# adaLN attention and FFN block on one core: prologue, epilogue and the place of the q and k projections re-ordered

## What is computed

```python
mod = (_silu(L0_c) @ L0_wmod).reshape(8, 6, 1, -1)
ga = (2 * (ga >= 0) - 1) * maximum(abs(ga), 0.25)  # gb likewise
h = _layernorm(x) * (1 + ca) + sa
q, k, v = (split_heads(lora_linear(h, ...)) for each)
scores = where(causal, q @ k.T / sqrt(16), -inf)
x = x + ga * lora_linear(softmax(scores) @ v, wo, ao, bo)
h = _layernorm(x) * (1 + cb) + sb
w = softmax of h @ Wg.T + bg, the two highest of 4 experts kept
expert_out[e] = relu(h @ Wi.T + h @ A[e].T @ B[e].T) @ Wo.T
x = x + gb * sum over e of w[e] * expert_out[e]
```

## Time and profile before

| | us |
|---|---|
| median of 3 runs | 1964.28 |
| lowest, highest | 1963.49, 1966.62 |
| the profiled execution | 1965.01 |
| its span, first to last instruction | 1963.3 |
| TensorE busy in it | 1801.6 (92%) |
| VectorE, ScalarE, GpSimd busy | 1239.0, 939.6, 530.5 |
| granted TensorE clock, mean | 0.967 |

### The profile page before, as it was taken

The page is one execution under the profiler, slowest core; times in us unless marked ns, Lnnn a source line. Parts: engine busy times, 40 slices in busy tenths (PEclk is TensorE's granted clock), DMA queues, the critical chain, the costliest instruction groups (busy, mean ns, idle before and its releaser), DMA issues. The chain is left out here.

```text
span 1963.3 us, 31621 instructions
## 1 busy us (share of the span) xinstructions
PE 1801.6 (92%) x10868; PEld 943.5 (48%) x10868; DVE 1239.0 (63%) x2681; ACT 939.6 (48%) x1701; POOL 530.5 (27%) x833
## 2 busy tenths in 40 slices
PE   7689879999989999899999999899999999799868
PEld 5334335454544555444554545445554545344535
DVE  3666677757686577666676576765777565863131
ACT  2145555544455445545455445554455454554320
POOL 2012112233223222233222232232222332133313
PEclk9579899999999999999999999999999999899979
DMA  7523243213322223223222233223222132120000
GB/s 177 145 50 87 51 87 83 70 40 78 85 60 71 56 64 87 70 38 92 63 71 70 40 85 70 72 58 82 47 60 79 31 88 63 39 39 25 25 1 22
DMA packets 249862, 128.69 MB, mean 66 GB/s; under 512 B 158214, under 2 KB 244834, under 8 KB 249708
## 3 DMA queue, kind: packets, MB, share of 16 engines
q1 hardware_dynamic: 245564, 125.61, 26.6%
q10 hardware_dynamic: 4144, 1.07, 0.4%
HBM read 83.06 MB, written 41.97 MB: 64 GB/s over the span
## 5 line engine op out<-in xcount | busy, mean ns | idle before, releaser
L1049 ACT ACTIVATE probs<-st 128x512 f32<-128x512 f32 (+1 forms) x1216 | 674.8, 576 | 705.2 <-PE st L896 703.1
L1314 DVE TENSOR_REDUCE negm<-mxs 128x1 f32<-128x384 f32 (+4 forms) x736 | 446.6, 617 | 243.3 <-PE mxs L884 239.1
L896 PE MATMUL st<-q_st,k_st 98*128 98x512 bf16 (+3 forms) x1536 | 452.3, 333 | 25.5 <-ACT probs L1049 18.3
L880 PE MATMUL mxs<-k_st,q_st 96*128 96x512 bf16 (+3 forms) x1280 | 408.1, 329 | 47.0 <-DVE negm_left L1314 26.7
L1314 DVE TENSOR_REDUCE negm_left<-mxs 128x1 f32<-128x512 f32 x512 | 345.2, 687 | 144.6 <-PE mxs L880 142.2
L911 PE MATMUL ov<-probs,v_g 128*32 128x512 f32 (+3 forms) x3072 | 333.2, 506 | 1.2 <-POOL probs L743 1.1
L880 PEld LDWEIGHTS mxs<-k_st,q_st 96*128 96x128 bf16 x1280 | 124.0, 98 | 300.8 <-DVE negm_left L1314 98.6
L855 PE MATMUL dense<-c_t,wi_t 128*128 128x512 f32 x512 | 263.9, 601 | 3.3 <-ACT ratio_b L1107 2.4
L756 POOL TENSOR_TENSOR hid<-hid,second 128x512 f32<-128x512 f32 x128 | 161.7, 1266 | 305.6 <-DVE second L1368 305.6
L896 PEld LDWEIGHTS st<-q_st,k_st 98*128 98x128 bf16 x1536 | 142.3, 99 | 169.1 <-ACT probs L1049 66.1
L740 POOL TENSOR_TENSOR fence<-fence 128x1 f32<-128x1 f32 x256 | 50.2, 196 | 613.8 <-ACT probs L1049 613.7
(11 more groups left out here) (165 smaller groups left out, 1696.4 us busy)
## 6 DMA issues: line engine op xcount, KB each, us to landing
q_st<-q_parts_scratch SPq DMA_DIRECT2D x384, 64.0 KB
k_st<-k_parts_scratch SPq DMA_DIRECT2D x384, 64.0 KB
q_parts_scratch<-q_part SPq DMA_DIRECT2D x16, 768.0 KB, 3.3
k_parts_scratch<-k_part SPq DMA_DIRECT2D x16, 768.0 KB, 5.2
xin<-in_L_attn_x SPq DMA_DIRECT2D x8, 1024.0 KB, 5.9
values_scratch<-v_rows SPq DMA_DIRECT2D x32, 256.0 KB, 2.1
v_g<-values_scratch SPq DMA_DIRECT2D x128, 64.0 KB, 3.9
x<-in_L_attn_x SPq DMA_DIRECT2D x16, 512.0 KB, 4.3
```

Of the source, the lines that this page charges most:

```text
L880: last = nc.tensor.matmul(mxs[:, bank_m, j * n:j * n + left], q_st[0:KS, slot, h0 + j, qt * P:(qt + 1) * P], k_st[0:KS, slot, h0 + j, k0:k ...
L896: last = nc.tensor.matmul(st[:, score_bank(ch, kt, h0), j * n:(j + 1) * n], k_st[0:KS + 2, slot, h0 + j, kt * P:(kt + 1) * P], q_st[0:KS + ...
L1049: nc.scalar.activation(probs[:, par, h0:h0 + heads, 0:n], st[:, score_bank(ch, kt, h0), 0:heads * n].rearrange("p (j q) -> p j q", q=n), A ...
L1314: nc.vector.tensor_reduce(dst[:, h0:h0 + heads], src, axis=AX.X, op=ALU.max, negate=True).then_inc(max_free, 1)
```

## The change

Three things are changed. **Prologue:** the norm of batch 0 (`ls1`, `ln1`) stands ahead of the gates' setup on VectorE; `ps` copies the parts of one half at a time (`ps00`, `ps01`), the first after two projections, and the first group's reads come ahead of the v rows 4 to 7; the maxima use the two score banks beside their own two (`max_room`). **Bodies:** all eight projection tiles stand among the FFN's tiles, four ahead of the first and four after the fifth (`PJ_UNITS` is empty); the copy of `ot` 0 is in unit 26, the load of `x1` in unit 37. **Epilogue:** the dense steps use all eight banks; the statistics of each quarter stand right behind its output projection; five FFN tiles' matmuls with the weights (`fa`, now both halves of the contraction) stand between the routing and the steps that need it, and from there five are kept ahead.

```diff
@@ body_plan @@
-        extra[PS_UNITS[0]] = ("ps", 0, 0)
-        extra[PS_UNITS[1]] = ("ps", 1, 0)
+        for ot in range(2):
+            begins[PS_UNITS[ot]] += [("ps", ot, 0, half) for half in range(2)]
...
-    extra[34] = ("xl", 0)
+    extra[37] = ("xl", 0)
...
-PJ_UNITS = (0, 6, 10, 11, 15)
-PJ_SLOTS = (5, 9, 13)
+PJ_UNITS = ()
+PJ_SLOTS = (0, 1, 2, 3, 9, 10, 11, 12)
-PS_UNITS = (17, 36)
+PS_UNITS = (26, 36)
@@ prologue_plan @@
-    plan = [("su", i) for i in range(N_PROJECTION_SETUP)]
-    plan += chain_steps(("ls1", "ln1")) + [("t1", i) for i in range(4)] + [("xin",)]
+    plan = [("su", 0)] + chain_steps(("ls1", "ln1")) + [("su", i) for i in range(1, N_PROJECTION_SETUP)]
+    plan += [("t1", i) for i in range(4)] + [("xin",)]
     values = [opened("va", i) for i in range(4)]
-    plan += values[0] + values[1] + pj[0] + [("ps", 0, 0)]
-    plan += values[2] + values[3] + [("rs", g, half, g) for g in range(2) for half in range(2)] + [("vg", 0)]
+    plan += values[0] + values[1]
+    for half in range(2):
+        plan += pj[0][4 * half:4 * half + 4] + [("ps", 0, 0, half)]
+    plan += [("rs", 0, half, 0) for half in range(2)] + values[2] + values[3]
+    plan += [("rs", 1, half, 1) for half in range(2)] + [("vg", 0)]
...
-    plan += [("ms",), ("ps", 1, 0), ("nm", 0)] + score_steps(0, *UNITS[0])
+    plan += [("ms",), ("nm", 0), ("ps", 1, 0, 0), ("ps", 1, 0, 1)] + score_steps(0, *UNITS[0])
@@ epilogue_plan @@
-    plan += [s for i in range(4) for s in opened("oa", i)]
-    plan += chain_steps(("ls2", "ln2")) + [("t2", i) for i in range(4)] + [("rt",), ("rx",)] + chain_steps(("ro",))
+    for i in range(4):
+        plan += opened("oa", i) + [("ls2", i)]
+    plan += chain_steps(("ln2",)) + [("t2", i) for i in range(4)] + [("rt",), ("rx",)] + chain_steps(("ro",))
+    tiles = [(half, ft) for half in range(2) for ft in range(8)]
+    plan += [("fa", *t) for t in tiles[:EARLY_TILES]]
     plan += [("mt", v) for v in range(2)] + [("rb", half) for half in range(2)]
     for half in range(2):
-        for ft in range(0, 8, 2):
-            plan += [(name, half, ft + i) for i in range(2) for name in ("fa", "fx")]
-            plan += [("fb", half, ft + i) for i in range(2)]
+        of_half = tiles[8 * half:8 * half + 8]
+        for i, t in enumerate(of_half):
+            plan.append(("fx", *t))
+            n = 8 * half + i - 2
+            if i >= 2:
+                plan.append(("fb", *tiles[n]))
+            if i >= 2 and n + EARLY_TILES < 16:
+                plan.append(("fa", *tiles[n + EARLY_TILES]))
+        for n in (8 * half + 6, 8 * half + 7):
+            plan.append(("fb", *tiles[n]))
+            if n + EARLY_TILES < 16:
+                plan.append(("fa", *tiles[n + EARLY_TILES]))
         plan += [s for t in range(4) for s in opened("wa", half, t)]
+EARLY_TILES = 5
+EPILOGUE_BANKS = 8
@@ adaln_block @@
+        banks = [dense[:, i, :] for i in range(DENSE_BANKS)] + [mxs[:, i, :] for i in range(MAX_BANKS)]
+        banks += [st[:, i, :] for i in range(SCORE_BANKS)] + [ov[:, :]]
+        def max_room(it):
+            spare = [st[:, i, :] for i in range(SCORE_BANKS)] if it < 0 else []
+            return [mxs[:, i, :] for i in range(MAX_BANKS)] + spare
...
-                    bank_m = done("mx") % MAX_BANKS
-                    after(pe, max_free, done("mx") - MAX_BANKS + 1)
+                    room = max_room(it)
+                    out = room[done("mx") % len(room)]
+                    after(pe, max_free, done("mx") - len(room) + 1)
...
                 elif kind == "fx":
                     half, ft = a
-                    hidden(db, 1, half, ft)
+                    if it < NB:
+                        hidden(db, 1, half, ft)
+                    elif (half, ft) == (0, 0):
+                        for i in range(EPILOGUE_BANKS):
+                            after(pe, dense_free[i], done(f"low bank{i}"))
```

More of the change, by code:

```diff
@@ L137, in body_plan @@
     extra = {}
+    begins = {u: [] for u in range(GROUPS * NU)}
     if post:
@@ L325, in tallied, with with_banks @@
     return names
-def with_banks(plan, first):
+def with_banks(plan, first, banks):
     n, steps, open_at = first, [], {}
@@ L333, in with_banks @@
         if s[0] in DENSE:
-            bank = next(i % DENSE_BANKS for i in range(n, n + DENSE_BANKS) if i % DENSE_BANKS not in open_at.values())
+            bank = next(i % banks for i in range(n, n + banks) if i % banks not in open_at.values())
             assert not (open_at and needs_all(s)), (s, open_at)
@@ L342, in with_banks @@
     assert not open_at
-    return steps, n % DENSE_BANKS
+    return steps, n % banks
 def needs_all(step):
@@ L378, in phase @@
                 counts["turned"] = counts["full"]
+            if s[0] in ("mt", "rb"):
+                counts[f"low bank{bank}"] = counts[f"bank{bank}"]
             if s[0] in ("vp", "rx", "t1"):
@@ L866, in run @@
                 db, db_b = dense_bank(bank)
+                if it == NB and kind == "ce":
+                    pe.wait_ge(exp_done, done("qk"))
+                    pe.wait_ge(max_free, done("mx"))
                 if kind == "mx":
@@ L1092, in run @@
                         act.wait_ge(blank_out, 16)
-                    after(act, parts_out[ot], done(f"ps{ot}") * (2 * 16))
+                    after(act, parts_out[ot][half], done(f"ps{ot}{half}") * (2 * 16))
                     nc.scalar.copy(dst[:, 0, :], db[:, :]).then_inc(part1_ready, 1)
```

56 lines of the change are left out of this document (33 added, 23 removed).

## The result

The changed kernel takes 1954.39 us (median of four runs, 1952.20 to 1954.59), against 1965.45 for the kernel before on the same chip (four runs, 1963.49 to 1967.87). By the medians it is 11.1 us faster (a quotient of 0.9944), where 12.2 were forecast, and inside the range of 1941 to 1962. The ratio that compares all runs of both kernels is 0.9927, with a 95% interval of 0.9902 to 0.9953; the quotient of the two medians lies inside it. It was profiled twice. The first profiled execution has a span of 1952.6.

The account below looks back on a forecast made before the run. TensorE was taken to bound attention beside the FFN, chains of single steps the epilogue's end. Terms -4.5, -5.1, +2.8 and -5.4 sum to -12.2, taking the median from 1964.3 to 1952.1 us; range 1941 to 1962.

Parts of the forecast that it names:

- Start of the maxima: Prologue: copying parts to DRAM by halves and the early norm let the reads and first maxima start earlier, -4.5 us.
- Four banks: Prologue maxima: with four banks VectorE runs through without bank waits, 26.6 us in place of 31.7, -5.1 us.
- 24.9 us of work, 0.7 until its first reduction, and about 1 us of seams: Prologue maxima: VectorE's busy time plus start and seams, giving a stretch of 26.6 us in place of 31.7.
- the rival that TensorE is the limit (3): Prologue maxima: TensorE at half clock is the limit, so four banks bring nothing; 1957 us in all, chance 0.06.
- Batches 1 to 6: Bodies: moving five projection tiles later costs +0.3 us per batch, with 1.0 for the clock +2.8 in all (-9 to +12).
- rival (2): Bodies: the clock falls in every batch around unit 14, costing 10 us in all; 1962 us, chance 0.12.
- rival (1): Units 10 to 14: v tiles don't fit under VectorE's chain, 3.0 us more per batch; 1970 us, slower, chance 0.07.
- if the clock row shows half speed in each batch: Bodies: a sign, named beforehand, that the prediction is wrong; no size of its own.
- keep their order: Batches 0 and 7: their order stays as before, so no gain or loss was counted for them.
- Epilogue: Epilogue: -5.4 us in all, from five FFN tiles done early, less +1.4 for later statistics and +3.8 of late waits.
- rival (4): Epilogue and bodies: GpSimd's backlog (3.4 us) and the bodies' losses (0.8 per batch) don't show; 1944 us, chance 0.15.

Follow-up runs that it names:

- the balanced run: Changed kernel with the epilogue's statistics behind all output projections again and later weight tiles split five and six over its halves: median 1950.18 us, ratio 0.9897.

## Why the prediction came out right, point by point

The stages of both kernels, from both pairs of profiles (first boundaries as in the text; us):

| | forecast | first pair | second pair |
|---|---|---|---|
| start of the maxima | -4.5 | 62.66 to 57.93: -4.7 | 62.47 to 58.53: -3.9 |
| maxima | -5.1 | 31.7 to 23.7: -8.0 | 31.7 to 24.6: -7.1 |
| from there to the end of batch 0 | 0 | -3.4 | -4.5 |
| batches 1 to 6 | +2.8 | +4.5 | +7.5 |
| batch 7 | 0 | +4.2 | +0.9 |
| epilogue | -5.4 | -3.2 | -7.2 |
| sum | -12.2 | -10.6 | -14.2 |

The total was right, and in part for reasons that it did not give.

**Start of the maxima: right.** Reads at 48.47 where the bounds were 48.5 and 49.9, first maxima at 57.93 where 58.1 stood. SP's own time was the bound, as the lower end had it: the reads start 0.74 us behind the last copy's issue. The half copies landed in 3.2 and 3.6 us (medians in that stretch), the whole k copy in 4.9. The page DMA: Bandwidth & Descriptors of the Trainium skill (the formula for one DMA) makes 2.9 of a half copy, by a fit to DMAs that GpSimd issues; these are SP's, two under way at a time, and the trace is 0.3 to 0.7 above it. The estimate by it, reads at 48.5 to 49, came true, but the landing did not decide it here; it did with the copies together, where the reads start 0.02 us behind the landing of the first half's k parts.

**Four banks: right mechanism, term too small by 2 to 3 us.** The step that failed is "24.9 us of work, 0.7 until its first reduction, and about 1 us of seams". It takes busy time for a floor. VectorE's reductions overlap in the records, which its timeline shows (two of 0.69 booked as 1.28, the next pair 1.20 later):

```profile
68.74 1.28 DVE L1360 TENSOR_REDUCE negm_left<-mxs 128x1 f32<-128x512 f32 x2
69.94 1.28 DVE L1360 TENSOR_REDUCE negm_left<-st 128x1 f32<-128x512 f32 x2
71.14 1.02 DVE L1360 TENSOR_REDUCE negm<-mxs 128x2 f32<-128x512 f32 x2
```

One reduction of 0.69 comes every 0.60, so the work is less than its busy sum, and the stretch ended 1 us below the 24.9 that stood as its least. The same 41 VectorE records that were busy for 24.89 us with waits between them are busy for 22.92 when they stand close. That the two banks were the cause the run with two banks shows, and the rival that TensorE is the limit (3), so that four banks bring nothing, is out: its 26.2 busy us were its half clock, 18.1 in the changed kernel at 0.86. That the clock would rise with the banks the prediction did not say.

**Batches 1 to 6: three ranges right, one wrong, and rival (2) came true.** Means over batches 1 to 6, per batch: units 0 and 1 -0.40 (forecast -0.4), 6 to 9 -1.09 (-1.0), 10 to 14 -6.20 (-5.5), 17 to 47 +7.70 (+8.1). Batch 7's units were a good model, with the v tiles wholly hidden in units 10 to 14: rival (1) is out. But units 15 and 16 were to be 0.85 shorter and are 0.73 longer. That is rival (2), "The clock falls in every batch around unit 14", which had 0.12 and 10 us in all; 1.6 per batch is 9.5. Half clock stood there for 6.8 to 10.2 us in all six batches, against 3.4 to 6.8 in four of them before (3.4 in four in its second profile). The prediction had named "if the clock row shows half speed in each batch" as a sign that it is wrong, and by that sign it was. That the total still came near is luck: units 10 to 14 and 17 to 47 gave 6 us more than forecast. The runs that put work into unit 15 (half clock mostly 3.4 us per batch, units 15 and 16 3.4 us shorter in all) and into 14 and 15 (no half clock at all) tie it to TensorE's idle time there. What exactly brings it is open: with the same wait of 1.68 us in unit 14 two of the six batches of the kernel before stayed at 1.00.

**Batches 0 and 7: "keep their order" failed as an argument.** Their plans are nearly unchanged, their time isn't. In batch 0 the load of x1, moved by three units, no longer stands ahead of the key reads on SP; putting it back brought 3.7 us in the units behind it. In batch 7 the reads for its first units came 2.1 us later, behind a store that the batch before issues later; that is 0.5 to 1.6 of its 4.2 us, and most of the rest is half clock that the first profile of before did not have and the second did. In neither case had I listed what stands behind the moved step on SP. What the Trainium skill says in DMA: Bandwidth & Descriptors (issuing engines are not separate DMA queues), that another issuing engine saves only issue time, was not tried here; what the reads lost on SP was the store's wait for its data (4.7 us for GpSimd's `ob` ahead of 1634.75), in which SP issues nothing.

**Epilogue: terms right, the base was not typical.** The statistics ended 1.2 later than the old order by the balanced run (1.4 forecast). The low-rank transposes came 3.3 us behind VectorE's end of the routing (4.0 forecast). From the first `fx` to the end of the last matmuls it took 57.9 (53.6 + 3.8 = 57.4 forecast), with the waits for GpSimd at the place that was named, so rival (4), in which they don't show, is out. The first `fx` itself stood 49.4 after the last product with v, where 47.5 was forecast: the output projections ran at half clock, so VectorE's first scaling came after 11.5 us and not after 7.6. Against a base in which they do so too, the new order is worth 7.1 to 7.2. The last matmul's end, 1959.6 in the sum, is 1959.8 by the earlier trace rows, which changes nothing. The mis-sized step is the base itself: it was one profile, with the clock at 1.00 from 1849 to 1867. The two other profiles of the old order have half clock there, and both take 117.9 us.

## What to carry to other kernels

Profile the base twice before costing a change against it: a stage whose length hangs on where a clock falls can differ by 4 us with no edit at all, and the forecast's terms are then measured against luck. Look, too, at where the profiled execution lies among its runs: in the bodies of before and in the tile in unit 15 it was the slowest of four, by 4 to 7 us. Fill the idle gaps of the engine that sets the pace before moving work away from them; units 0 and 6 gave back 0.4 and 1.1 us of a tile's 1.72, and the emptied unit 15 cost half clock besides. Look at the longest single idle time there, not at the sum: a tile that cut it from 1.68 to about 0.9 us was worth 3.0 us with the sum no smaller. Of every load or store that moves by a few steps, list what is queued behind it on its issuing engine, in the batches whose plan did not change too.
